# GpSimd in place of VectorE for the low input parts and layer 0's sums, inside a gated recurrence

## The chip, the cores and the metric

The kernel runs on one core of one Trainium2 chip. The metric is the device time of one execution in microseconds (us), taken as the median of several runs; less is better. All times of the profile are microseconds from the start of the span unless ns is written.

## What is computed

Two layers act on x, 4 batches x 512 positions x 256 features. Cut to the part that the change touches:

```
step(h, x_t):                                  # layer 0, a gated recurrence over 512 positions
    z  = sigmoid(x_t W_z + h U_z + vz)
    r  = sigmoid(x_t W_r + h U_r + vr)
    hh = tanh(x_t W + (r * h) U + vh)
    h  = (1 - z) * h + z * hh
hist  = all h                                  # 4 x 512 x 256
blk   = gelu(hist W1 + b1) W2 + b2             # where the router selects the position, else hist
x     = x + (blk or hist)                      # so the kernel needs x + blk and x + hist
x     = x + layer 1 (a 4-expert block, then a 64-expert block, 8 chosen per row)
```

## The kernel before, in words

**Stages.** The program runs in four stages: the recurrence (`gru`, to about 1056 us, with a short set-up before its first step at 21 us), the 4-expert block (`dense`), the routing, and the 64 experts (`experts`, to the end). The change touches `gru` alone.

**The recurrence.** Positions are walked one at a time by a loop over j, on all engines, in 13 windows of 40 steps (the last, window 12, has 32). In the code a window is called a span, and jj is the step's offset in it. The state is feature-major: 128 partitions x 8 values (2 halves of the features x 4 batches). To multiply in half the time a float32 product is split into a high and a low float16 (or float32r) part. One step is a ring of small instructions that wait for each other:

- TensorE (`recur`, L869) makes the r gate's sum from step_high and step_low, the z gate's from the state (`raw`), the candidate's from rh_high and rh_low, and the kept part of the next step's r from keep_part: 48 products of 128x128 by 4 columns. Between them it works through prepared products: one of the next window's input product (L838) at most steps and some of the feed-forward block of the previous window (L882, L897).
- ScalarE forms r (L510), z (L512 to L515) and the candidate (L517), then a larger piece: seeding the next window's banks (L503), GELU, block output (L447), the history copy (L495).
- VectorE forms rh_high (L768) and rh_low (a scan, L630), the kept part (L775, L777, L781), step_high (L785), step_in (L786), step_low (L630), the new state (L794, L799, L801, L805). Each reads two operands in SBUF. After L805 it may do one larger piece that is placed by hand at given offsets.

**The pieces that the change moves.** All are VectorE `tensor_tensor` instructions on one half of the features, [128, 4 batches, 40 positions], placed behind L805 of a step:

- `low_inputs(span, pieces)` (L553 to L556): the low part of the next inputs, x minus its high part, into x_part[1]. In window w the two for window w+2 are made at offsets 7 and 8 (13 and 17 in window 0), behind ScalarE's high part (L420) of offset 4 (10). The two for window 1 are made in the set-up (L569, L570). TensorE waits for them at offset 0 of the window before their own (L945), a whole window after they were made.
- `add_to_block(span, d)` (L701 to L704): blk += x, in window w for w-2, at offsets 36 and 37, behind ScalarE's block output (L447) of offsets 2 and 3. In window 12 at 20, 21 and, for window 11, at 27, 28.
- `add_state(span, d)` (L706 to L710): xT += hist, at offsets 38, 39 (22, 23 and 29, 30 in window 12), behind the adds to the block and the history copies. The results are read in the next stage alone.

There are 24 instructions of each kind, 72 together. `layer_sums` (L712 to L727) holds the offsets of the last two. GpSimd, in this stage, sets six constants at the start (L530 to L537) and is idle until the routing.

The step in which one such piece stands, in VectorE's program:

```
last of the step:  scalar_tensor_tensor(out=part_of(1, j), in0=h_new, ..., in1=part_of(0, j))   # L805
lows = LOW_AT if span else FIRST_LOW_AT                                                         # L807
if span + 2 < SPANS and jj in lows: wait_ge(s_xhi, span + 2); low_inputs(...)                   # L808
ffn_vector(span, jj)                                # sums, hidden splits, weight parts          # L811
next step's first: wait_ge(s_r, m); rh_high = (r + 1) * h                                       # L767
```

Of the kernel before, what the change touches and what calls it, by code (L numbers as in the profile page):

```python
# [6 lines left out]
F32 = mybir.dt.float32  # L7
# [4 lines left out]
ALU = mybir.AluOpType  # L12
# [5 lines left out]
KD = D // P  # L18
# [5 lines left out]
SEG = 16  # L24
# [186 lines left out]
def gru(nc, sem, A, bank, xT, hist, ident, ones, ones_bf, condT, slot_row, s_x, s_const, load_ffn_up, load_ffn_down, load_next,  # L211
        up_loaded, down_loaded, shared_loaded, raw, shared_parts, under, ffn_sems, wr, wr_rep, idle_rows):

    with ExitStack() as own:
        def t(name, shape, dt=F32):
            return own.enter_context(nc.sbuf_tensor(name, shape, dt))

        w16_1, w16_2, h_steps, hid16, full16, blk, x_last, fsc, silu_c, b1, b2 = under
        STARTS = tuple(range(0, S, SPAN))
        LENGTHS = tuple(min(SPAN, S - at) for at in STARTS)  # L220
        SPANS = len(STARTS)
        FINAL = SPANS - 1
# [8 lines left out]
        x_part = [t(f"in_part{p}", [P, KD, B, S], F32R) for p in range(2)]  # L231
# [29 lines left out]
        s_xhi, s_xlo = sem("inputs_high"), sem("inputs_low")  # L261
# [15 lines left out]
        s_hist = sem("hist_copied")  # L277
# [4 lines left out]
        s_fup, s_gelu, s_fhi, s_flo, s_fdn, s_blk = ffn_sems  # L282
        s_silu = sem("cond_silu")
        s_bx = sem("inputs_added_to_block")
# [5 lines left out]
        FIRST_HIGH_AT, FIRST_LOW_AT = TERMS + B, (13, 17)  # L290
        HIGH_AT, LOW_AT = 4, (7, 8)
# [10 lines left out]
        def steps_of(v, span):  # L302
            return v[:, :, :, STARTS[span]:STARTS[span] + LENGTHS[span]]

        def place(j):
            return j // SPAN, j % SPAN
# [39 lines left out]
        ADD_BLOCK_AT, ADD_STATE_AT = (36, 37), (38, 39)  # L346
        ADD_BLOCK_FINAL_AT, ADD_STATE_FINAL_AT = (20, 21), (22, 23)
        ADD_BLOCK_LAST_AT, ADD_STATE_LAST_AT, KEEP_LAST_AT = (27, 28), (29, 30), 20
# [39 lines left out]
        with nc.Block() as block:  # L388
            @block.sync
            def _(sp):  # L390
                for g, (w, u, c, b) in enumerate(names):
                    sp.dma_start(C[:, g], A["L0_cond_" + c].rearrange("(k p) e -> p k e", p=P)).then_inc(s_cw[g], 16)
                for g, (w, u, c, b) in enumerate(names):
                    sp.dma_start(W[:, g], A["L0_cond_" + w].rearrange("(k p) e -> p k e", p=P)).then_inc(s_w[g], 16)
                for g, (w, u, c, b) in enumerate(names):
                    sp.dma_start(U[:, g], A["L0_cond_" + u].rearrange("(k p) e -> p k e", p=P)).then_inc(s_uw, 16)
                load_ffn_up(sp)
                for k in range(KD):
                    sp.dma_start(xT[:, k, :, EARLY:S],
                                 A["xT"][k * P:(k + 1) * P, :].rearrange("p (b s) -> p b s", b=B)[:, :, EARLY:S]).then_inc(s_x, 16)  # L400
                sp.dma_start(slot_row[:], A["slot_row"]).then_inc(s_const, 16)
                load_ffn_down(sp)
                sp.wait_ge(s_x, 32)
                sp.wait_ge(s_const, 16)
                sp.wait_ge(s_w16lo, 2 * PAIRS * LOWS)
                load_next(sp)
# [124 lines left out]
            def _(pool):  # L531
# [4 lines left out]
                nc.gpsimd.memset(idle_rows[:], 0.0)  # L536
                nc.gpsimd.memset(lift[:], 2.0 ** (STATE_EXP - 1)).then_inc(s_set, 1)  # L537

            @block.vector
            def _(dve):  # L540
                nc.vector.memset(ring[:, 2 * SEG - 1], 0.0).then_inc(s_h, 1)
# [8 lines left out]
                dve.sem_inc(s_hr, 1)  # L550
                dve.sem_inc(s_slo, 1)

                def low_inputs(span, pieces):  # L553
                    for k in pieces:
                        nc.vector.tensor_tensor(steps_of(x_part[1], span)[:, k], steps_of(xT, span)[:, k],
                                                steps_of(x_part[0], span)[:, k].bitcast(F32), ALU.subtract).then_inc(s_xlo, 1)  # L556

                def low_weights(g):
                    dve.wait_ge(s_whi, g + 1)
                    nc.vector.tensor_tensor(W_part[1][:, g], W[:, g], W_part[0][:, g].bitcast(F32), ALU.subtract).then_inc(s_wlo, 1)  # L560
# [5 lines left out]
                    last = nc.vector.tensor_reduce(peak[:, g:g + 1], U[:, g].rearrange("p k e -> p (k e)"), AX.X, ALU.max,  # L566
                                                   apply_absolute_value=True)
                last.then_inc(s_peak, 1)
                dve.wait_ge(s_xhi, 1)  # L569
                low_inputs(1, range(KD))  # L570
                dve.wait_ge(s_v, 2)
                nc.vector.tensor_copy(bias[:], bank[1][:, GATES * C2:GATES * C2 + GATES * KD]).then_inc(s_bias, 1)
                dve.wait_ge(s_bias, 1)
# [124 lines left out]
                        nc.vector.scalar_tensor_tensor(out=low, in0=whole, scalar=fsc[:, 13:14], in1=high,  # L698
                                                       op0=ALU.mult, op1=ALU.subtract).then_inc(s_flo, 1)

                def add_to_block(span, d):  # L701
                    dve.wait_ge(s_blk, 2 * KD * span + d + 1)
                    v = steps_of(blk, span)[:, d]
                    nc.vector.tensor_tensor(v, v, steps_of(xT, span)[:, d], ALU.add).then_inc(s_bx, 1)  # L704

                def add_state(span, d):  # L706
                    dve.wait_ge(s_bx, span * KD + d + 1)
                    dve.wait_ge(s_hist, -(-(STARTS[span] + LENGTHS[span]) // SEG))
                    v = steps_of(xT, span)[:, d]
                    nc.vector.tensor_tensor(v, v, steps_of(hist, span)[:, d], ALU.add)  # L710

                def layer_sums(window, jj):  # L712
                    for d in range(KD):
                        if window == FINAL:
                            if jj == ADD_BLOCK_FINAL_AT[d]:
                                add_to_block(window - 2, d)
                            if jj == ADD_STATE_FINAL_AT[d]:
                                add_state(window - 2, d)
                            if jj == ADD_BLOCK_LAST_AT[d]:
                                add_to_block(window - 1, d)  # L720
                            if jj == ADD_STATE_LAST_AT[d]:
                                add_state(window - 1, d)
                        elif window >= 2:
                            if jj == ADD_BLOCK_AT[d]:
                                add_to_block(window - 2, d)
                            if jj == ADD_STATE_AT[d]:
                                add_state(window - 2, d)  # L727

                def ffn_vector(window, jj):
                    layer_sums(window, jj)  # L730
                    if window == 0:
                        scale_step(fsc.bitcast(U32), jj)
                    for f in range(KH):
                        for part in range(2):
                            if window == FINAL and jj == SPLIT_FINAL_AT[f][part]:
                                split_hidden((window - 1) * KH + f, part)
                            if 1 <= window < FINAL and jj == SPLIT_AT[f][part]:
                                split_hidden((window - 1) * KH + f, part)
                    for at in range(2 * PAIRS * LOWS):
                        if (window, jj) == FFN_LOW_AT[at]:  # L740
                            i, n = at // LOWS, at % LOWS
                            whole, high, low = ffn_piece(i, n)
                            c = 6 + i // PAIRS
                            dve.wait_ge(s_w16hi, i + 1)
                            nc.vector.scalar_tensor_tensor(out=low, in0=whole, scalar=fsc[:, c:c + 1], in1=high,
                                                           op0=ALU.mult, op1=ALU.subtract).then_inc(s_w16lo, 1)
                    if (window, jj) in SHARED_LOW_AT:
                        i, n = SHARED_LOW_AT.index((window, jj)) // LOWS, SHARED_LOW_AT.index((window, jj)) % LOWS
                        whole, high, low = shared_piece(i, n * LOW, (n + 1) * LOW)
                        dve.wait_ge(s_nhi, i + 1)  # L750
                        nc.vector.tensor_tensor(low, whole, high.bitcast(F32), ALU.subtract).then_inc(s_nlo, 1)
                    if window == 2 and jj in (21, 22):
                        k = jj - 21
                        nc.vector.tensor_copy(wr_rep[:, k], wr[:, k:k + 1].to_broadcast([P, P]))
                    if (window, jj) == (2, 36):
                        nc.vector.tensor_scalar(half_c[:], condT[:], 0.5, None, ALU.mult).then_inc(s_silu, 1)
                    if (window, jj) == (2, 37):
                        dve.wait_ge(s_silu, 2)
                        nc.vector.scalar_tensor_tensor(out=silu_c, in0=turn_c[:], scalar=1.0, in1=half_c[:],
                                                       op0=ALU.add, op1=ALU.mult).then_inc(s_silu, 1)  # L760

                for j in range(S):
                    h, h_new = ring[:, (j - 1) % (2 * SEG)], ring[:, j % (2 * SEG)]
                    m = j + 1
                    span, jj = place(j)
# [30 lines left out]
                    if j % SEG == 0 and j >= 2 * SEG:  # L796
# [7 lines left out]
                    dve.wait_ge(s_hhi, m + 1)  # L804
                    nc.vector.scalar_tensor_tensor(out=part_of(1, j), in0=h_new, scalar=2.0, in1=part_of(0, j),  # L805
                                                   op0=ALU.mult, op1=ALU.subtract).then_inc(s_hlo, 1)
                    lows = LOW_AT if span else FIRST_LOW_AT  # L807
                    if span + 2 < SPANS and jj in lows:  # L808
                        dve.wait_ge(s_xhi, span + 2)
                        low_inputs(span + 2, (lows.index(jj),))  # L810
                    ffn_vector(span, jj)  # L811
                    if j == 0:
                        low_recurrent(GATES - 1)
# [1206 lines left out]
```

## Time and profile before

| | us |
|---|---|
| median of 3 runs | 2133.65 (2133.19 to 2134.84) |
| the profiled execution: span | 2133.2 |
| the profiled execution: its own time | given by its span alone; it lies 0.45 under the median |
| recurrence (first gate r to the last) | 20.8 to 1053.8 |
| engines busy, share of the span | PE 98%, PEld 92%, DVE 74%, ACT 48%, POOL 19% |

PE is TensorE's matmuls, PEld its weight loads (they overlap), DVE VectorE, ACT ScalarE, POOL GpSimd. A row of the timeline is: start, duration, engine, line, operation, output<-inputs, shapes, count, and in brackets the idle time of the engine before it with what ended it. A row with a count over 1 merges neighbours, so its duration is the stretch that they cover. Pipelined instructions can start before the one ahead has ended.

### The profile page before, as it was taken

The numbers are of one execution on the slowest core, as the hardware profiler recorded it, in microseconds if no ns is written. First come the engines' busy times: TensorE is split into PE (matmuls) and PEld (weight loads), VectorE is DVE, ScalarE is ACT, GpSimd is POOL, SyncE is SP. The second block draws the span as 40 slices with busy tenths as digits, with TensorE's granted clock in tenths as the row PEclk, the third lists the DMA queues.
The fourth block names the chain that finished last, engine by engine and source line by source line (L and its number), as shares of the span: only waits on it lengthen the run. The fifth ranks groups of instructions, "written<-read, shape, count | busy, mean of one in ns | idle before, by whom it ended". The sixth has DMA issues, their size and how long they took to land. (4 is left out here: it accounts for less than half of the span.)

```text
span 2133.2 us, 82927 instructions
## 1 busy us (share of the span) xinstructions
PE 2095.2 (98%) x32732; PEld 1968.5 (92%) x32732; DVE 1572.5 (74%) x8995; ACT 1025.5 (48%) x3981; POOL 415.7 (19%) x560
## 2 busy tenths in 40 slices
PE   8999999999999999999999999999999999999997
PEld 7899999999999999999768888767999999999997
DVE  6887877787777887787745555593777777777775
ACT  3565565665555565656555776533222222222221
POOL 0000000000000000000000000445455555555553
PEclk6555555555555555555599999999999999999998
DMA  3001000000000000000002322223888888888882
GB/s 127 4 4 44 4 4 4 4 4 4 4 4 4 4 4 4 4 4 4 3 1 92 111 84 80 107 70 133 299 268 276 278 267 276 279 268 277 278 264 58
DMA packets 55558, 213.72 MB, mean 100 GB/s; under 512 B 11578, under 2 KB 40960, under 8 KB 46976
## 3 DMA queue, kind: packets, MB, share of 16 engines
q1 hardware_dynamic: 36276, 184.41, 23.5%
q0 software_dynamic: 17408, 23.61, 5.9%
q8 instruction: 257, 4.21, 0.8%
q14 instruction: 133, 1.09, 0.2%
q10 hardware_dynamic: 1484, 0.40, 0.1%
HBM read 192.82 MB, written 15.57 MB: 98 GB/s over the span
## 5 line engine op out<-in xcount | busy, mean ns | idle before, releaser
L1891 PE MATMUL bank<-xe,ring 128*128 128x160 f32 x3072 | 438.8, 299 | 0.7 <-DVE xe L1949 0.7
L1891 PEld LDWEIGHTS bank<-xe,ring 128*128 128x128 f32 x3072 | 422.7, 190 | 0.9 <-issue 0.9
L1942 DVE STREAM_TRANSPOSE turned<-ye 32x64 f32<-32x64 f32 x1240 | 291.5, 235 | 16.2
L869 PEld LDWEIGHTS bank<-keep_part,Us 128*128 128x128 f16 x6120 | 276.0, 111 | 1.6 <-DVE keep_part L781 0.4
L1659 POOL MEMSET cum<- 128x320 f32 x1 | 0.4, 365 | 1349.7 <-POOLq L1051 1349.7
L869 PE MATMUL bank<-keep_part,Us 128*128 128x4 f16 x6120 | 259.3, 170 | 0.4 <-DVE keep_part L781 0.3
L1927 ACT ACTIVATE gate_f<-bank 128x160 f32<-128x160 f32 x384 | 116.4, 303 | 284.7 <-PE bank L1891 283.7
L869 PE MATMUL bank<-raw,Us 128*128 128x4 f16 x6132 | 241.3, 167 | 0.5 <-DVE raw L805 0.4
L1833 POOL DMA_INDIRECT out_rows<-res,to_row x128 | 192.3, 1503 | 227.2 <-DVE res L1961 193.9
L510 ACT ACTIVATE r_h<-bank 128x8 f32<-128x8 f32 x512 | 92.8, 181 | 278.9 <-PE bank L869 278.4
L1902 PE MATMUL bank<-mid,ring 128*128 128x160 f32 x1536 | 219.1, 299 | 0.0
L1902 PEld LDWEIGHTS bank<-mid,ring 128*128 128x128 f32 x1536 | 212.1, 190 | 0.0
L1972 DVE TENSOR_TENSOR mid<-bank,gate_f 128x160 f32<-128x160 f32 x384 | 117.6, 318 | 126.1 <-ACT gate_f L1927 120.3
L869 PEld LDWEIGHTS bank<-raw,Us 128*128 128x128 f16 x6132 | 209.8, 105 | 0.8 <-DVE raw L805 0.6
L869 PE MATMUL bank<-rh_high,Us 128*128 128x4 f16 x4088 | 206.7, 173 | 3.3 <-issue 0.6
L838 PE MATMUL bank<-in_part,W_part 128*128 128x160 f32 (+1 forms) x432 | 206.9, 479 | 1.0 <-DVE bank L612 1.0
L869 PE MATMUL bank<-step_high,Us 128*128 128x4 f16 x4088 | 189.0, 168 | 4.5 <-DVE step_high L785 1.5
L869 PEld LDWEIGHTS bank<-rh_high,Us 128*128 128x128 f16 x4088 | 165.4, 112 | 23.2 <-DVE rh_high L768 11.1
L515 ACT ACTIVATE z_cand<-tz,lift 128x8 f32<-128x8 f32 x512 | 155.8, 304 | 16.5
L869 PEld LDWEIGHTS bank<-step_high,Us 128*128 128x128 f16 x4088 | 148.1, 105 | 9.1 <-DVE step_high L785 3.0
L785 DVE TENSOR_TENSOR step_high<-z_cand 128x8 f16<-128x8 f32 x512 | 89.5, 175 | 81.4 <-ACT z_cand L517 74.5
L1126 PE MATMUL bank<-x_part,weights_part 128*128 128x512 f32 x576 | 137.0, 396 | 2.2 <-DVE x_part L1317 2.2
(279 smaller groups left out, 4051.4 us busy)
## 6 DMA issues: line engine op xcount, KB each, us to landing
ring<-in_ew SPq DMA_DIRECT2D x64, 2304.0 KB, 9.2
raw<-in_L_cond_ew SPq DMA_DIRECT2D x16, 1024.0 KB, 6.2
ctx_rows<-rows SPq DMA_DIRECT2D x2, 1280.0 KB, 7.0
dense_w<-in_L_ffn_W SPq DMA_DIRECT2D x2, 1024.0 KB, 9.3
dense_w<-in_L_cond_sw SPq DMA_DIRECT2D x2, 1024.0 KB, 6.3
out_rows<-res,to_row POOLq DMA_INDIRECT x128, 4.8
xT<-in_xT SPq DMA_DIRECT2D x2, 864.0 KB, 10.7
dense_w<-in_sw1T SPq DMA_DIRECT2D x1, 1536.0 KB, 11.1
```

Source lines behind the costliest of these rows:

```text
L510: nc.scalar.activation(r, pre_of(0, q, jj), ACT.Tanh, scale=inv[0]).then_inc(s_r, 1)
L515: nc.scalar.activation(z, tz[:], ACT.Identity, scale=2.0 ** (STATE_EXP - 1), bias=lift[:, 0:1]).then_inc(s_z, 1)
L785: nc.vector.tensor_tensor(step_high[:, :, 2], z, cand, ALU.mult).then_inc(s_shi, 1)
L838: last = nc.tensor.matmul(product(span, n), W_part[w][:, g, k, m * P:(m + 1) * P], steps_of(x_part[x], span)[:, k], start=(k == 0 and i == ...
L869: last = nc.tensor.matmul(pre[g][q][:, jj, m, :], Us[:, g, p, k, m * P:(m + 1) * P], x[part][:, k * B:(k + 1) * B], start=False, stop=Fals ...
L1126: last = nc.tensor.matmul(up[f % len(up)][:], w[i][:, k, f * P:(f + 1) * P], x[j][:, k], start=(k == 0 and i == 0 and j == 0), stop=(k == ...
L1833: nc.gpsimd.indirect_dma_start(out=out[:, :], out_offset=bass.IndirectOffsetOnAxis(ap=to_idx[c][:, 0:1], axis=0), in_=res[e % 2][c][:], in ...
L1891: last = nc.tensor.matmul(bank[f % UPS][:, s_ * CAP:(s_ + 1) * CAP], w1[u][:, k, s_ * FFN + f * P:s_ * FFN + (f + 1) * P], xe[e % 2][:, k] ...
L1902: last = nc.tensor.matmul(bank[6 + e % 2][:, d * CAP:(d + 1) * CAP], w2[u][:, f, d * P:(d + 1) * P], mid[e % 2][:, f], start=(f == 0), sto ...
L1927: nc.scalar.activation(gate[:, f % 2], bank[f % UPS][:, CAP:2 * CAP], ACT.Silu).then_inc(s_silu, 1)
L1942: last = nc.vector.transpose(y[:, :, q, :], ye[e % 2][q * SQ:(q + 1) * SQ, :, j * SQ:(j + 1) * SQ])
L1972: nc.vector.tensor_tensor(mid[e % 2][:, f], bank[f % UPS][:, 0:CAP], gate[:, f % 2], ALU.mult).then_inc(s_mid, 1)
```

## The change

The 72 instructions go from VectorE's program to GpSimd's, unchanged in operation and shape. On VectorE the waits and pieces at hand-placed offsets disappear. On GpSimd they stand in one loop over windows, in this order: in each window w the two low parts for w+2, then (from w = 2) the two adds to the block and the two adds of the state for w-2; in window 12 those for 10 and for 11. Each is held only by its semaphores, by no offset.

```diff
--- before
+++ after
@@ gpsimd @@
                 nc.gpsimd.memset(lift[:], 2.0 ** (STATE_EXP - 1)).then_inc(s_set, 1)
+                def low_inputs(span):
+                    pool.wait_ge(s_xhi, span)
+                    for k in range(KD):
+                        nc.gpsimd.tensor_tensor(steps_of(x_part[1], span)[:, k], steps_of(xT, span)[:, k],
+                                                steps_of(x_part[0], span)[:, k].bitcast(F32), ALU.subtract).then_inc(s_xlo, 1)
+                def add_to_block(span, d):
+                    pool.wait_ge(s_blk, 2 * KD * span + d + 1)
+                    v = steps_of(blk, span)[:, d]
+                    nc.gpsimd.tensor_tensor(v, v, steps_of(xT, span)[:, d], ALU.add).then_inc(s_bx, 1)
+                def add_state(span, d):
+                    pool.wait_ge(s_bx, span * KD + d + 1)
+                    pool.wait_ge(s_hist, -(-(STARTS[span] + LENGTHS[span]) // SEG))
+                    v = steps_of(xT, span)[:, d]
+                    nc.gpsimd.tensor_tensor(v, v, steps_of(hist, span)[:, d], ALU.add)
+                low_inputs(1)
+                for window in range(SPANS):
+                    if window + 2 < SPANS:
+                        low_inputs(window + 2)
+                    for span in ((window - 2,) if 2 <= window < FINAL else (window - 2, window - 1) if window == FINAL else ()):
+                        for d in range(KD):
+                            add_to_block(span, d)
+                        for d in range(KD):
+                            add_state(span, d)
@@ vector @@
-                def low_inputs(span, pieces): ...
-                dve.wait_ge(s_xhi, 1)
-                low_inputs(1, range(KD))
-                def add_to_block(span, d): ...
-                def add_state(span, d): ...
-                def layer_sums(window, jj): ...
                 def ffn_vector(window, jj):
-                    layer_sums(window, jj)
...
-                    lows = LOW_AT if span else FIRST_LOW_AT
-                    if span + 2 < SPANS and jj in lows:
-                        dve.wait_ge(s_xhi, span + 2)
-                        low_inputs(span + 2, (lows.index(jj),))
                     ffn_vector(span, jj)
```

## Rows read from the trace of the kernel before

**Rows 1.** The page: the span, and TensorE's granted clock in 40 slices.
```profile
span 2133.2 us, 82927 instructions
...
PEclk6555555555555555555599999999999999999998
```

**Rows 2.** Windows, 80 us of recurrence: busy us of each engine (count), granted clock, DMA.
```profile
500.00:580.00 80.00, 79.89 (x2034) 78.62 (x2031) 63.93 (x502) 48.35 (x241) 0.00 (x0) 0.50 0.02 4
```

**Rows 3.** Timeline of window 5, two steps.
```profile
441.68 0.18 ACT L510 ACTIVATE r_h<-bank 128x8 f32<-128x8 f32 x1 [0.57 <-PE bank L869]
441.82 0.29 PEld L838 LDWEIGHTS bank<-in_part,W_part 128*128 128x128 f32 x1
...
441.89 0.17 DVE L768 SCALAR_TENSOR_TENSOR rh_high<-r_h,ring 128x8 f16<-128x8 f32 x1 [0.24 <-ACT r_h L510]
...
442.12 0.33 PEld L869 LDWEIGHTS bank<-rh_high,Us 128*128 128x128 f16 x8
...
442.61 0.55 PEld L869 LDWEIGHTS bank<-keep_part,Us 128*128 128x128 f16 x12
...
442.90 0.18 DVE L785 TENSOR_TENSOR step_high<-z_cand 128x8 f16<-128x8 f32 x1 [0.16 <-ACT z_cand L517]
...
443.13 0.29 PEld L869 LDWEIGHTS bank<-step_high,Us 128*128 128x128 f16 x8
...
443.57 0.32 DVE L555 TENSOR_TENSOR in_part<-xT,in_part 128x160 fp32r<-128x160 f32 x1
443.68 0.18 ACT L510 ACTIVATE r_h<-bank 128x8 f32<-128x8 f32 x1 [0.57 <-PE bank L869]
...
443.89 0.17 DVE L768 SCALAR_TENSOR_TENSOR rh_high<-r_h,ring 128x8 f16<-128x8 f32 x1
...
445.67 0.18 ACT L510 ACTIVATE r_h<-bank 128x8 f32<-128x8 f32 x1 [0.22 <-PE bank L869]
```

**Rows 4.** Groups of VectorE, whole span: busy us, mean ns | idle before.
```profile
L710 DVE TENSOR_TENSOR xT<-xT,hist 128x160 f32<-128x160 f32 x24 | 7.8, 324 | 0.0
L704 DVE TENSOR_TENSOR ffn_out<-ffn_out,xT 128x160 f32<-128x160 f32 x24 | 7.6, 318 | 0.0
L555 DVE TENSOR_TENSOR in_part<-xT,in_part 128x160 fp32r<-128x160 f32 (+1 forms) x24 | 7.5, 316 | 0.0
```

**Rows 5.** Timeline of the routing stage: GpSimd alone, and beside a VectorE instruction.
```profile
1353.04 2.35 POOL L1663 TENSOR_TENSOR context_part<-hist,context_part 128x1024 fp32r<-128x1024 f32 x1 [0.80 <-ACT context_part L1606]
...
1358.43 1.27 POOL L1667 TENSOR_TENSOR shared_part<-dense_w,shared_part 128x512 fp32r<-128x512 f32 x1 [0.57 <-ACT shared_part L1609]
1358.59 1.66 DVE L1711 TENSOR_TENSOR left<-rows,st 128x512 f32<-128x512 f32 x1
...
1364.44 0.69 DVE L1711 TENSOR_TENSOR left<-rows,st 128x512 f32<-128x512 f32 x1
```

**Rows 6.** The same timeline later: both engines with instructions back to back.
```profile
1370.77 1.47 POOL L1676 TENSOR_TENSOR act_f<-act_f,lin 128x512 f32<-128x512 f32 x1
1371.13 1.14 DVE L1725 TENSOR_SCALAR st<-st 128x8 f32<-128x8 f32 x1
1372.21 1.29 POOL L1667 TENSOR_TENSOR shared_part<-dense_w,shared_part 128x512 fp32r<-128x512 f32 x1
...
1372.43 1.61 DVE L1727 TENSOR_TENSOR gates<-gates,left 128x512 f32<-128x512 f32 x1
...
1373.45 1.74 POOL L1676 TENSOR_TENSOR act_f<-act_f,lin 128x512 f32<-128x512 f32 x1
...
1380.89 0.17 DVE L1725 TENSOR_SCALAR st<-st 128x8 f32<-128x8 f32 x1
```

**Rows 7.** Timeline of the set-up, before the first step.
```profile
10.56 0.45 ACT L420 ACTIVATE in_part<-xT 128x320 fp32r<-128x320 f32 x1
...
12.26 1.87 DVE L566 TENSOR_REDUCE peak<-U 128x1 f32<-128x512 f32 x3 [1.70 <-DMA U<-in_L_cond_U]
```

More of the change, by code:

```diff
@@ L551, in _ @@
                 dve.sem_inc(s_slo, 1)
[L553 to L556, printed above, removed]
                 def low_weights(g):
@@ L699, in split_hidden @@
                                                        op0=ALU.mult, op1=ALU.subtract).then_inc(s_flo, 1)
[L701 to L727, printed above, removed]
                 def ffn_vector(window, jj):
-                    layer_sums(window, jj)
                     if window == 0:
```

## The prediction

> **What bounds the kernel now.** I read the page first: the span is 2133.2 us, and TensorE's granted clock is 0.5 to 0.6 for the first 20 of 40 slices [rows 1], which is the 1.2 GHz level; that is the recurrence. Then the busy time by stretch: in 80 us there TensorE is busy 79.89 and its weight loads 78.62, while VectorE is busy 63.93, ScalarE 48.35 and GpSimd nothing [rows 2]. So the recurrence looks bound by TensorE's queue, with VectorE 80% busy and GpSimd free. But a ring of dependent instructions can be as tight as a full queue, and a share doesn't tell which, so I read the timeline of two steps next [rows 3]. A step lasts from one r gate to the next: 441.68 to 443.68 is 2.00 us, 443.68 to 445.67 is 1.99.
>
> Two hand-overs in it decide. **rh_high:** r is ready at 441.68 + 0.18 = 441.86, VectorE's L768 starts at 441.89 and ends at 442.06; TensorE's weight load of the input product ends at 441.82 + 0.29 = 442.11 and rh_high's start at 442.12. So TensorE is the later one, by 0.05. **step_high:** VectorE's L785 ends at 442.90 + 0.18 = 443.08; TensorE's keep_part loads end at 442.61 + 0.55 = 443.16 and step_high's start at 443.13, as one stretch begins while the other is draining. TensorE is later by 0.05 to 0.08; I take 0.05. So TensorE sets the step, but VectorE is only about 0.05 behind it at two places. VectorE waits for data twice in the step, 0.24 before L768 and 0.16 before L785 [rows 3]. These 0.40, and 0.05 at each hand-over, are all the room there is: 0.5 us in a step of 2.0. A VectorE held up for longer holds up the ring, since everything that TensorE could do instead stands behind the waiting product in its own queue.
>
> **The change, part by part.**
>
> *What VectorE loses.* 72 instructions, 24 each of 0.316, 0.318 and 0.324 us [rows 4], 22.9 us in all. What are they worth on the path? L555 at 443.57 ends at 443.89, and L768 behind it starts at 443.89, 0.03 after r (443.86). In the step before, with no such piece, L768 also starts 0.03 after r (441.86 to 441.89), and the two steps take 2.00 and 1.99 [rows 3]. The piece fits exactly into the wait for r. So I take the gain at 0. Its upper bound is the whole 22.9 if no piece were hidden, which the two steps speak against; the lower is nothing.
>
> *What GpSimd gains: its own time.* No row has this instruction at 128x160 on GpSimd. The nearest are the same operation at 1024 columns, 2.35 us, and at 512, 1.27 us, both with no VectorE instruction of two inputs ahead of them [rows 5]. That is 1.08 us for 512 columns, 2.1 ns a column, and 0.19 us at no columns; 160 columns are 0.19 + 0.34 = 0.53 us. Lower bound 0.34 (no fixed part), upper bound the 1.27 of the 512-column row, because four short rows of 40 may run worse than one long row. I take 0.53. GpSimd is idle here, so 72 x 0.53 = 38 us of its time cost nothing by themselves.
>
> The Trainium skill, GPSIMD Engine Reference, section 3.1, gives `tensor_tensor` on GpSimd at 1.96 times VectorE's time. On VectorE's 0.32 [rows 4] that makes an estimate of 0.62, by which the sum below would be 35.7 instead of 29.4 us.
>
> *What it does to VectorE.* This is the term that decides. Where the engines meet in the routing, L1711 takes 0.69 us alone and 1.66 beside a GpSimd instruction: that one ends at 1358.43 + 1.27 = 1359.70, and L1711 ends at 1360.25, 0.55 later. It stood still until GpSimd was done and then ran [rows 5]. A small one fares the same: L1725, 128x8, takes 0.17 alone and 1.14 when issued at 1371.13 beside a GpSimd instruction that ends at 1372.24 [rows 6]. With both queues full they take turns: GpSimd's ends at 1373.50, L1727 runs and ends at 1374.04, and GpSimd's next, issued at 1373.45, takes 1.74 instead of 1.29, having waited 0.45 for it [rows 6]. So one GpSimd instruction holds one VectorE instruction for up to its whole length, and gives way to one in between.
>
> The Trainium skill, SBUF (State Buffer), "Practical consequences", says that a VectorE instruction with two SBUF inputs contends with a GpSimd instruction that reads SBUF, and that the one behind blocks fully. All twelve VectorE instructions of a step are of that kind, though the rows show the hold for `tensor_tensor` and a `tensor_scalar` alone.
>
> *When they run.* On GpSimd nothing is held by an offset. ScalarE's high input part at offset 4 releases the two low parts; the adds to the block wait for block outputs of offsets 2 and 3, already there, and the history copies are long done. So in each of windows 2 to 10 **six instructions run in one burst**, 3.18 us of GpSimd; windows 0 and 1 have bursts of two; window 11 has one at offset 2 and three at offset 3; window 12 twice that pattern. With VectorE's small instructions taking turns, a burst of six meets six to eight of them, about half to one step of its program. Of each burst the room of one step, 0.5 us, is hidden; a lone instruction gets one wait and hand-over of it, about 0.25. The sum:
> - windows 2 to 10: 9 x (3.18 - 0.5) = 24.1
> - windows 0 and 1: 2 x (1.06 - 0.5) = 1.1
> - window 11: (0.53 - 0.25) + (1.59 - 0.5) = 1.4; window 12: 2.8
> - the two of the set-up: 0. ScalarE's part is ready at 10.56 + 0.45 = 11.01, and VectorE waits for a load until 12.26 [rows 7], 1.25 us, which covers 1.06. If that load came early, they would cost up to 1.06.
>
> Together **29.4 us**. With 0.34 us for one it is 70 x 0.34 - 7.7 = 16.1, with 1.27 it is 81.2; 7.7 is the hidden part of the sum.
>
> *Waits added.* GpSimd's waits hold nothing else: behind them in its queue stand only more pieces. TensorE needs the low parts a window (80 us) later, the sums are read after the recurrence, and the last of them can start once the block output at offset 26 of window 12 is done, five steps (10 us) before its end. No DMA moves.
>
> **The number.** The sum is made on the profiled execution: 2133.2 + 29.4 = 2162.6 us. It lies 0.45 under the median of the runs, so I give 2133.65 + 29.4 = 2163.0.
>
> **Rivals.**
> - *A, the forecast: a full hold, taking turns.* 2163. For it: three holds in the rows, among them a 128x8, and a turn given and taken [rows 5, 6]. Chance 0.72.
> - *B, GpSimd gets in only at VectorE's waits.* VectorE's instructions follow each other closely, and GpSimd may only enter where VectorE has stopped for r or for the candidate. Then each holds 0.53 - 0.24 - 0.05 = 0.24 before L768 or 0.53 - 0.16 - 0.05 = 0.32 before L785; 70 times 0.28 is 19.6, a time of 2153. For it: VectorE's queue is denser here than in the rows. Against: between L768 and its scan, before L781 and elsewhere it also stops briefly for its own results. Chance 0.13.
> - *C, not slower: the short instructions aren't held.* If a hold needs VectorE instructions that stream many columns (the only two-input ones in the rows have 512 and more), 8 columns of input may slip through. The place is L768 and L785 beside GpSimd; it decides below a hold of 0.05 to 0.25 an instruction, where the room swallows it. Then the time is 2133.6, and if the removed pieces delayed L768 by 0.03 after all, 70 x 0.03 = 2.1 less, 2131.5. To gain over 0.2% it would need 0.06 for each of 70. The 1.14 of L1725 [rows 6] speaks against. Chance 0.10, of which 0.03 for over 0.2% faster.
> - *D, the piece is dearer on GpSimd.* Past 0.77 us for one (four rows of 40 instead of one) the loss is 70 x 0.77 - 7.7 = 46.2 and more, 2180 or above. Nothing in the rows shows such a shape. Chance 0.05.
>
> **How the numbers follow.** The likeliest is A. The range takes in B and A with prices from about 0.34 to 0.77 for one: 2133.65 + 16.1 is 2149.8, less a few us if a burst hides two steps' room instead of one; 2133.65 + 46.2 is 2179.9. So 2146 to 2180, leaving out C and D. A measurement of this kernel can tell about 0.2%, 4.3 us. Slower by over that: A, B and D, 0.90. Within: 0.07 of C. Faster: 0.03.
>
> **What would show it.** In the profile after: GpSimd busy by some 38 us more, 72 instructions at 0.53 or a little longer for waiting their turn; six in a row after offset 4 of windows 2 to 10; beside them VectorE's small instructions at 0.5 to 0.7 us instead of 0.17; one or two steps per window that take 2.7 us longer together, and all others at 2.00. VectorE's summed busy time would rise, not fall. The stages after the recurrence keep their length. Wrong if L768, L785 and the scans keep 0.17 to 0.21 us beside GpSimd (C), if only those behind a wait grow (B), or if a burst is much over 4.2 us long (D). If steps free of GpSimd's work fall clearly below 1.99 us where a piece stood, the removed pieces were not hidden, and my zero for the gain was wrong.

## The result: 12.7 us slower, and the profile after

The changed kernel takes 2146.22 us (median of 4 runs, 2145.77 to 2149.28) against 2133.49 for the kernel before. The ratio is 1.0059, with a 95% interval of 1.0047 to 1.0071: 12.7 us slower, where 29.4 were forecast. The direction was right, the size more than twice too large, and the median stands at the very bottom of the range.

The page of the kernel after, with the lines that answer to [rows 1]:

```profile
span 2147.5 us, 82919 instructions
...
PEclk6555555555555555555599999999999999999998
```

This execution was the longest of the four, 2149.28 us, so 1.8 us lie outside its span. (In runs of the kernel before it is 2.0; so the execution profiled before took about 2135.2 us and lay over the median, not 0.45 under it, which the forecast, made from the median, does not hang on.) Its span is 14.3 us longer than that of before. By the L510 rows the recurrence runs from 20.94 to 1067.98, 1047.04 us, against 20.83 to 1053.80, 1032.97: 14.1 of the 14.3 us are in the recurrence. The clock there is still the lower of the two levels.

The runs of the kernel before lie near two levels, 2131 and 2134.5 us, so beside each median below I also give the length of the recurrence in the profiled execution (1032.97 before, 1047.04 after). It is the steadier measure: no version changes anything behind the recurrence, yet the rest of the span lies anywhere between 1096.0 and 1101.2 us in the twelve traces.

Window, as [rows 2], and the groups of GpSimd that took the place of [rows 4]:

```profile
500.00:580.00 80.00, 79.34 (x2014) 77.33 (x2012) 63.12 (x489) 46.94 (x235) 2.98 (x6) 0.50 0.02 4
```

```profile
L554 POOL TENSOR_TENSOR xT<-xT,hist 128x160 f32<-128x160 f32 x24 | 12.3, 531 | 0.0
L542 POOL TENSOR_TENSOR in_part<-xT,in_part 128x160 fp32r<-128x160 f32 (+1 forms) x24 | 12.2, 525 | 821.5 <-ACT in_part L420 821.5
L548 POOL TENSOR_TENSOR ffn_out<-ffn_out,xT 128x160 f32<-128x160 f32 x24 | 12.1, 518 | 201.1 <-ACT ffn_out L447 201.1
```

GpSimd's price was read rightly: 0.518 to 0.531 us each against 0.53, although each instruction here works on four short rows of 40 columns. In these 80 us VectorE gave up 0.8 us of busy time, not the six pieces' 1.9, although half a step less fell into them: the instructions beside GpSimd grew. Over the whole span its busy time went from 1572.5 to 1573.7 us, so 22.9 us of pieces left and as much came back.

This is the burst of window 5, timeline of VectorE, ScalarE's r gate, GpSimd and some weight loads, as [rows 3]. The step before it takes 1.99, the one behind it 2.03.

```profile
442.27 1.03 POOL L542 TENSOR_TENSOR in_part<-xT,in_part 128x160 fp32r<-128x160 f32 x2 [78.80 <-ACT in_part L420]
442.34 0.50 DVE L792 SCALAR_TENSOR_TENSOR r_h<-keep,step_in 128x8 f32<-128x8 f32 x1
...
442.65 0.18 ACT L510 ACTIVATE r_h<-bank 128x8 f32<-128x8 f32 x1 [0.46 <-PE bank L856]
442.76 0.15 DVE L796 SCALAR_TENSOR_TENSOR raw<-ring,raw 128x8 f16<-128x8 f32 x1
442.86 0.47 DVE L759 SCALAR_TENSOR_TENSOR rh_high<-r_h,ring 128x8 f16<-128x8 f32 x1
442.97 0.19 PEld L856 LDWEIGHTS bank<-raw,Us 128*128 128x128 f16 x4 [0.23 <-DVE raw L796]
...
443.26 0.99 POOL L548 TENSOR_TENSOR ffn_out<-ffn_out,xT 128x160 f32<-128x160 f32 x2
...
443.36 0.48 DVE L650 TENSOR_TENSOR_SCAN rh_low<-r_h,rh_high 128x24 f16<-128x24 f32 x1
...
443.77 0.52 DVE L766 SCALAR_TENSOR_TENSOR keep_part<-nz,ring 128x8 f16<-128x8 f32 x1
...
444.21 0.15 DVE L768 SCALAR_TENSOR_TENSOR keep<-nz,ring 128x8 f32<-128x8 f32 x1
...
444.23 1.02 POOL L554 TENSOR_TENSOR xT<-xT,hist 128x160 f32<-128x160 f32 x2
...
444.47 0.31 DVE L772 TENSOR_TENSOR keep_part<-keep,keep_part 128x8 f16<-128x8 f32 x1
444.70 0.16 DVE L776 TENSOR_TENSOR step_high<-z_cand 128x8 f16<-128x8 f32 x1
444.78 0.50 DVE L777 SCALAR_TENSOR_TENSOR step_in<-z_cand 128x8 f32<-128x8 f32 x1
...
445.45 0.18 PEld L856 LDWEIGHTS bank<-step_low,Us 128*128 128x128 f16 x4 [0.22 <-DVE step_low L650]
...
445.75 0.18 ACT L510 ACTIVATE r_h<-bank 128x8 f32<-128x8 f32 x1 [1.36 <-PE bank L856]
```

Six GpSimd instructions in a row, six VectorE instructions grown: L792, L759, the scan, L766, L772 and L777, by 0.34, 0.30, 0.27, 0.35, 0.14 and 0.34 over the 0.16, 0.17, 0.21, 0.17, 0.17 and 0.16 that they take elsewhere. That makes **1.74 us of holds, 0.29 each**. The step from 442.65 to 445.75 takes 3.10 and the next 2.03, so 1.13 us of the 1.74 reach the step and 0.6 are hidden. In windows 3 to 9 the step of offset 5 takes 3.10 or 3.11, in window 10, with short last inputs, 2.91. A held instruction ends just behind GpSimd's: GpSimd's second, fourth and sixth end at 443.30, 444.25 and 445.25, and L759, L766 and L777 at 443.33, 444.29 and 445.28. Between two held instructions others run at full speed: L796, L768 and L776 each end within 0.15 or so of the start of GpSimd's next. GpSimd isn't slowed by them: six in a row take 442.27 to 445.25, 0.50 each.

### The profile page after: what moved, and what is told of

The parts are those of the page before. It is cut to its first block and busy times, and to the rows that moved or that the text cites. A ratio compares the mean times of both kernels' runs of the same rounds, so it can differ in the third digit from the quotient of the medians.

```text
span 2147.5 us, 82919 instructions
## 1 busy us (share of the span) xinstructions
PE 2101.3 (98%) x32724; PEld 1969.6 (92%) x32732; DVE 1573.7 (73%) x8923; ACT 1025.5 (48%) x3981; POOL 451.5 (21%) x632
## 5 line engine op out<-in xcount | busy, mean ns | idle before, releaser
L510 ACT ACTIVATE r_h<-bank 128x8 f32<-128x8 f32 x512 | 92.7, 181 | 284.4 <-PE bank L856 283.9
L542 POOL TENSOR_TENSOR in_part<-xT,in_part 128x160 fp32r<-128x160 f32 (+1 forms) x24 | 12.2, 525 | 821.5 <-ACT in_part L420 821.5
L776 DVE TENSOR_TENSOR step_high<-z_cand 128x8 f16<-128x8 f32 x512 | 89.0, 174 | 78.9 <-ACT z_cand L517 70.5
```

Of the source, the lines that this page charges most:

```text
L510: nc.scalar.activation(r, pre_of(0, q, jj), ACT.Tanh, scale=inv[0]).then_inc(s_r, 1)
L776: nc.vector.tensor_tensor(step_high[:, :, 2], z, cand, ALU.mult).then_inc(s_shi, 1)
```

## The experiments

The kernel before took 2133.98 us (24 runs) beside the sums alone, the low parts alone, the halves and the run without sums; 2131.63 (13 runs) beside the merged pairs, the copies and the run released by L794; and 2134.45 (17 runs) beside the memsets and the two runs released by L805.

**The parts alone.** First the sums alone on GpSimd (low parts back at their offsets on VectorE):

```diff
-                low_inputs(1)                      # GpSimd
                 for window in range(SPANS):
-                    if window + 2 < SPANS:
-                        low_inputs(window + 2)
```

> Only the 48 sums go to GpSimd; the low parts of the inputs stay on VectorE. Theory 1 (GpSimd's instruction holds VectorE's port only for its column part, about 0.34 of its 0.53 us; what isn't swallowed by the room in a step lengthens it): windows 2 to 11 each have one instruction at offset 2 and three at offset 3, as window 11 of the changed kernel, which lost about 1.1 us; 10 x 1.1 and 2.0 in window 12 make 13 us over the kernel before. Theory 2 (the whole 0.53 us holds, and more is hidden than I counted, some 2 us of every burst): a burst of three or four, 1.6 to 2.1 us, is hidden all but whole; 0 to 4 us over before.

Measured: 2144.41 us, ratio 1.0042 (1.0025 to 1.0059), 10.4 us over before; recurrence 1042.97, 10.0 over: nearer to theory 1's 13 than to theory 2's 0 to 4. Then the low parts alone (`layer_sums` back on VectorE):

```diff
                     if window + 2 < SPANS:
                         low_inputs(window + 2)     # GpSimd
-                    for span in (...): add_to_block, add_state
```

> Only the 24 low parts of the inputs go to GpSimd, two behind each other in windows 0 to 10; the sums stay on VectorE at their offsets. Theory 1: 2 x 0.34 less little; window 1 of the changed kernel, with the same two, lost 0.6; 11 x 0.6 is 7 us over before. Theory 2 (2 us of a burst hidden): 1.06 us is hidden whole, 0 to 1 us over before.

Measured: 2136.68, ratio 1.0013 (1.0003 to 1.0023), 2.7 us over; recurrence 1038.21, 5.2 over (the rest of this execution's span is 3.3 us shorter than that of before). The sums carry most of the loss: one instruction at the end of offset 2 makes the step of offset 3 2.28, and the three behind it make the step of offset 4 2.81 in windows 4 to 9, 1.1 us together. Two low parts make one step 2.28 in windows 3 to 9, and 2.48 to 2.62 in windows 1, 2 and 10. So in most windows a pair costs 0.3, four 1.1 and six 1.1: not additive. For the low parts alone theory 1 had said 7 us and theory 2 at most 1; the recurrence lies between them. Why a pair is cheap is seen in this timeline of the run with low parts alone, window 5 (next r gates at 440.36 and 442.64, as the step is 2.28):

```profile
439.98 1.03 POOL L542 TENSOR_TENSOR in_part<-xT,in_part 128x160 fp32r<-128x160 f32 x2 [79.64 <-ACT in_part L420]
440.04 0.50 DVE L816 SCALAR_TENSOR_TENSOR r_h<-keep,step_in 128x8 f32<-128x8 f32 x1
...
440.46 0.15 DVE L820 SCALAR_TENSOR_TENSOR raw<-ring,raw 128x8 f16<-128x8 f32 x1
440.57 0.47 DVE L783 SCALAR_TENSOR_TENSOR rh_high<-r_h,ring 128x8 f16<-128x8 f32 x1
...
440.78 0.29 PEld L849 LDWEIGHTS bank<-in_part,W_part 128*128 128x128 f32 x1
```

The first hold, 0.34, makes the state's low part (L820) late, and with it TensorE, whose queue has reached the input product 0.3 late (440.78). The second hold, 0.30 on rh_high, ends at 441.04, before that product's load is done at 441.07. Two holds fall on two sides of the same 0.3 and are paid once.

**What holds: GpSimd's time or its columns.** Each instruction cut in two, over two batches each:

```diff
-    for k in range(KD): tensor_tensor(...[:, k], ...)
+    for k in range(KD):
+        for b in range(0, B, 2): tensor_tensor(...[:, k, b:b + 2], ...)    # all three kinds; TensorE waits for twice the count
```

> The changed kernel with each GpSimd instruction cut in two of two batches (80 columns, about 0.36 us each by the intercept of 0.19): the same columns in 144 instructions. Theory 1 (hold by columns, the fixed part free): the loss stays near 12.7 us, at most a few us less. Theory 2 (whole instruction holds): GpSimd's time of a burst of six grows from 3.2 to 4.3 us, and the loss with it to about 24 us.

Measured: 2140.57, ratio 1.0031 (1.0020 to 1.0041), 6.6 us over; recurrence 1041.37, 8.4 over. Timeline of its window 5, in part (GpSimd at 439.68, 440.96 and 442.26, four in each row), and the group:

```profile
439.68 1.32 POOL L543 TENSOR_TENSOR in_part<-xT,in_part 128x80 fp32r<-128x80 f32 x4 [77.40 <-ACT in_part L420]
...
439.75 0.33 DVE L795 SCALAR_TENSOR_TENSOR r_h<-keep,step_in 128x8 f32<-128x8 f32 x1
...
440.73 0.30 DVE L769 SCALAR_TENSOR_TENSOR keep_part<-nz,ring 128x8 f16<-128x8 f32 x1
...
442.60 0.36 DVE L762 SCALAR_TENSOR_TENSOR rh_high<-r_h,ring 128x8 f16<-128x8 f32 x1
```

```profile
L543 POOL TENSOR_TENSOR in_part<-xT,in_part 128x80 fp32r<-128x80 f32 (+1 forms) x48 | 15.7, 355 | 808.5 <-ACT in_part L420 808.5
```

GpSimd works 30% longer (47.4 us in the three groups against 36.6), and the loss of a burst halves: two steps of 2.32 and 2.28 instead of 3.10 and 2.03. In the whole recurrence it falls from 14.1 to 8.4 us. Theory 2 falls. Theory 1 has the sign, but promised "a few us less" at most. The other way, each pair made one of 320 columns (`add_to_block` and `add_state` over both halves at once):

> The changed kernel with each pair of GpSimd instructions made one over both feature halves (320 columns, about 0.87 us by 0.19 + 320 x 0.0021): the same columns in 36 instructions. Theory 1 (hold by columns): three holds of 0.68 instead of six of 0.34, loss near 12.7 us or a few us above, since a long hold overruns the room. Theory 2 (whole instruction holds): GpSimd's time of a burst falls from 3.2 to 2.6 us, and the loss to about 7 us.

Measured: 2149.63, ratio 1.0079 (1.0062 to 1.0096), 18.0 us over the 2131.63 beside it (15.6 over 2134); recurrence 1048.36, 15.4 over. GpSimd's three groups together are shorter (31.3 us) and the loss is a little larger, not near theory 2's 7 us. The timeline of window 5:

```profile
442.68 0.89 POOL L541 TENSOR_TENSOR in_part<-xT,in_part 128x320 fp32r<-128x320 f32 x1 [79.05 <-ACT in_part L420]
...
442.80 0.80 DVE L793 SCALAR_TENSOR_TENSOR raw<-ring,raw 128x8 f16<-128x8 f32 x1
```

The hold is 0.80 - 0.17 = 0.63. With 80, 160 and 320 columns GpSimd's instruction takes 0.36, 0.53 and 0.87 us and holds a short VectorE instruction for up to 0.19, 0.35 and 0.68. **The hold is at most its length less 0.16 to 0.19**: in the traces with GpSimd's `tensor_tensor` in the recurrence a held short instruction ends 0.02 to 0.07 behind GpSimd's, so nearly all of its own 0.17 passes under the hold. The same columns in smaller portions fit better between the waits.

**Reading or any work.** On the kernel before, six copies of 160 columns (one input) in windows 0 to 10, then in their place six memsets:

```diff
+for window in range(SPANS - 2):
+    pool.wait_ge(s_xhi, window + 2)
+    for i in range(6):
+        ...                                        # waits for the last but one of its own writes
+        nc.gpsimd.tensor_copy(spare[:, n % 2], C[:, 0, 0, 0:160])     # second run: memset(spare[:, n % 2], 0.0)
```

> The kernel before, with six copies of 160 float32 columns on GpSimd (one input) in the same places. If the hold is for reading: VectorE's instructions beside them are held, by less than for two inputs, since the copy is shorter; some us over before. If only two-input instructions of GpSimd hold: 2133.5.

Measured: 2137.58, ratio 1.0019 (1.0009 to 1.0029); recurrence 1035.64, 2.7 over; the step of offset 5 takes 2.30 in most windows.

> The kernel before, with six memsets of 320 bfloat16 columns on GpSimd (about 0.35 us each, they read nothing) to a spare tile behind ScalarE's high input part in windows 0 to 10, beside the six copies of the run before, 0.32 us each with one input, which lengthened the step of offset 5 by 0.30. If the hold is for reading the state buffer: no such step, 2.00 there, and the time of the kernel before. If any work of GpSimd, its writes or its semaphores hold VectorE: again 0.3 us a window.

Measured: 2134.43, ratio 0.9998 (0.9989 to 1.0007); recurrence 1034.41. Its 1.4 us over before are not at offset 5, where the step takes 2.00 against 1.99 to 2.00: they are a few thousandths of a us in each of hundreds of steps, most of them without memsets, and their cause is open. These memsets have 320 columns, as a tile for 384 did not fit into SBUF and that version gave no time. First the copies, then the memsets:

```profile
439.93 0.57 POOL L547 COPY spare<-C 128x160 f32<-128x160 f32 x2
439.96 0.30 DVE L785 SCALAR_TENSOR_TENSOR keep_part<-nz,ring 128x8 f16<-128x8 f32 x1
440.19 0.34 DVE L787 SCALAR_TENSOR_TENSOR keep<-nz,ring 128x8 f32<-128x8 f32 x1
```

```profile
437.82 0.97 POOL L546 MEMSET spare<- 128x320 bf16 x3
437.87 0.17 DVE L784 SCALAR_TENSOR_TENSOR keep_part<-nz,ring 128x8 f16<-128x8 f32 x1
437.95 0.16 DVE L786 SCALAR_TENSOR_TENSOR keep<-nz,ring 128x8 f32<-128x8 f32 x1
```

Beside copies VectorE's instructions grow by 0.13 and 0.18; beside memsets, which write as many bytes, they keep 0.17 and 0.16. So GpSimd's reads hold VectorE, its writes, waits and semaphores don't. The Trainium skill, SBUF (State Buffer), "Practical consequences", says just this of a VectorE instruction with two SBUF inputs and GpSimd's reads and writes; the trace agrees, for instructions of 8 columns too.

**Where in the step.** Every GpSimd instruction in a step of its own, at VectorE's old offsets, released by L794 (L785 in the changed kernel) of that step; then released by L805; then by L805 in halves, at offsets 7 to 10 and 30 to 37 (in window 12 elsewhere, the last eight two a step):

```diff
-    (six in a row as their data come)
+    for each step with a piece:
+        pool.wait_ge(s_hhi, j + 2)        # L794's; then s_hlo, L805's; then s_hlo with halves, each in a step of its own
+        one piece
```

> The changed kernel with every GpSimd instruction put into a step of its own, at the offsets that VectorE had, released by the step's L785 (s_hhi), so that it runs from about 1.75 us into the step, over VectorE's wait for r. Theory 1 (the column part at the end holds): it starts about 0.45 before the next rh_high, so it holds VectorE 0.05 to 0.1 beyond it, of which 0.05 is room; 70 x 0.05 is 3 us over before. Theory 2 (whole instruction holds from its start): L792 and L796 are held too, and the loss is near that of 70 lone instructions, 0.2 each, 14 us.

Measured: 2155.27, ratio 1.0106 (1.0090 to 1.0123); recurrence 1053.43, 20.5 over, more than either theory had (3 and 14 us). It is the slowest of all: steps of 2.34 behind the low parts and the last of the sums, 2.26 behind the others.

```profile
449.83 0.52 POOL L542 TENSOR_TENSOR in_part<-xT,in_part 128x160 fp32r<-128x160 f32 x1 [16.12 <-DVE raw L795]
...
449.86 0.51 DVE L806 SCALAR_TENSOR_TENSOR raw<-ring,raw 128x8 f16<-128x8 f32 x1
...
450.43 0.18 PEld L866 LDWEIGHTS bank<-raw,Us 128*128 128x128 f16 x4 [0.28 <-DVE raw L806]
```

L794 is followed so closely by the rest that GpSimd started just before the state's low part was issued. That instruction (L805 before, L806 here), which I had counted as free, is the one held (0.51 for 0.17), and TensorE stands 0.28 us for it.

> The changed kernel with every GpSimd instruction (160 columns) in a step of its own, released by the step's last VectorE instruction (L805, s_hlo) rather than by L794. Theory 1, put now as: VectorE's instruction is held until GpSimd's ends, less the 0.15 to 0.2 us that it takes anyway. GpSimd's starts at about 0.04 after L805's end and ends 0.53 later, some 0.2 after the place where rh_high would have ended; less 0.05 of room that is 0.15 for each, 10 us in all; steps of 2.15 to 2.2. The state's low part is not held, as it was in the run released by L794 (steps of 2.34). If the hold ended before the instruction does, the steps stay at 2.00 to 2.05.

Measured: 2146.70, ratio 1.0059 (1.0044 to 1.0074); recurrence 1047.79, 14.8 over, where 10 had been expected. Steps with a piece take 2.20, as expected, or 2.13 in window 10; the others take what they take in the changed kernel.

```profile
449.44 0.17 DVE L806 SCALAR_TENSOR_TENSOR raw<-ring,raw 128x8 f16<-128x8 f32 x1
449.64 0.18 ACT L510 ACTIVATE r_h<-bank 128x8 f32<-128x8 f32 x1 [0.57 <-PE bank L866]
449.69 0.52 POOL L542 TENSOR_TENSOR in_part<-xT,in_part 128x160 fp32r<-128x160 f32 x1 [16.00 <-DVE raw L806]
...
449.85 0.39 DVE L769 SCALAR_TENSOR_TENSOR rh_high<-r_h,ring 128x8 f16<-128x8 f32 x1 [0.24 <-ACT r_h L510]
```

GpSimd ends at 450.21 and rh_high at 450.24, where it would have ended at 450.02: held 0.22, less a little room, 0.20 a step as expected.

> The same with each instruction cut in two of 80 columns (0.36 us), each half in a step of its own behind L805. Theory 1: a half ends about where rh_high would have ended, 0.24 us of VectorE's wait for r cover it; the steps stay at 2.00 to 2.03, the time within 0.1% of the kernel before although GpSimd does all 72 pieces in 144 instructions. If each GpSimd instruction had a price of its own whatever its place (semaphores, dispatch), 144 of them would cost more than the 72 of the changed kernel, 13 us and over. No version is expected to beat the kernel before by more than 0.1%, as the pieces were hidden there too.

Measured: 2139.97, ratio 1.0028 (1.0017 to 1.0039), 5.5 us over; recurrence 1038.69, 5.7 over. The steps of offsets 8 to 11, behind the low parts, take 2.03 or 2.04, as expected. Those of offsets 31 and 33 take 2.11 instead of their usual 2.03: there VectorE still has a larger piece behind L805, and GpSimd's half takes 0.43 and ends later. I had not multiplied either: 140 halves at 0.04 on average are the 5.7 us that "within 0.1%" left out. In the rows of offset 7 GpSimd starts 0.08 after L805's end, not 0.04, and rh_high takes 0.23 instead of 0.17.

```profile
445.94 0.36 POOL L542 TENSOR_TENSOR in_part<-xT,in_part 128x80 fp32r<-128x80 f32 x1 [20.00 <-DVE raw L803]
...
446.10 0.23 DVE L766 SCALAR_TENSOR_TENSOR rh_high<-r_h,ring 128x8 f16<-128x8 f32 x1 [0.24 <-ACT r_h L510]
```

**What removal from VectorE is worth.** The kernel before without the sums anywhere (`layer_sums(window, jj)` deleted):

> The kernel before without the 48 sums of layer 0 (no adds to the block or to the state; this part is left out on every engine). Both theories: the pieces were hidden on VectorE, so the time stays at that of the kernel before within 0.1%. If it falls by 5 us or more, my zero for the gain is wrong and the loss on the other side is larger than 12.7 us.

Measured: 2130.78, ratio 0.9986 (0.9976 to 0.9995), 3.2 us less; recurrence 1030.96, 2.0 less: a little more than the 0.1% that was allowed for. The median step at offsets 36 to 39, where the sums stood, is 2.01 with and without them. So the sums are hidden in their steps, and what is gained is small and lies elsewhere, in the steps of 2.1 to 2.3 that are scattered over the recurrence of every run.

These steps go with VectorE's program, not with GpSimd's work. Over windows 1 to 12 the same 25 steps are over 2.09 in the three kernels that have VectorE's program of before (before, copies, memsets). In the six that have that of the changed kernel, whatever GpSimd does, the same 29 are in all six, of which only 4 are among those 25; without the sums anywhere there are 16. In several of them VectorE stands idle for 0.22 to 0.30 us for nothing that the profile shows. This is the step of offset 7 of window 5, which takes 2.34, in the changed kernel and in the one released by L805:

```profile
447.93 0.17 DVE L796 SCALAR_TENSOR_TENSOR raw<-ring,raw 128x8 f16<-128x8 f32 x1 [0.30 <-issue]
```

```profile
447.45 0.17 DVE L806 SCALAR_TENSOR_TENSOR raw<-ring,raw 128x8 f16<-128x8 f32 x1 [0.30 <-issue]
```

Why VectorE stops there is open. But the six kernels allow a sum that leaves GpSimd out: each step at the shortest that it takes in any of them adds up to a recurrence of 1033.12, against 1032.97 before. So by this estimate taking the pieces from VectorE gained nothing, and 13.9 of the 14.1 us are lost in steps that GpSimd lengthens.

## Why the prediction had the direction right and the size wrong

- **TensorE sets the step, VectorE close behind; the removed pieces gain nothing.** Right: by the estimate above the recurrence without them, and without GpSimd's work, is as long as before to 0.15 us. The run without the sums gained 2.0 us there, but not in their steps.
- **GpSimd's own time, 0.53 us.** Right: 0.518 to 0.531. The rival of a dearer piece and the estimate of 0.62 from the Trainium skill's ratio (GPSIMD Engine Reference, section 3.1) were both too high; the ratio is 0.53 / 0.32 = 1.65 here.
- **It holds VectorE, six in a burst, at offset 5, and two or fewer steps carry it.** Right. `scalar_tensor_tensor`, the scan and a `tensor_tensor` of 8 and 24 columns are held, so the rival in which short instructions slip through is out, and so is the one in which GpSimd gets in only at VectorE's waits: L766 and L777 were held in the middle of a run of instructions. That one or two VectorE instructions run between two held ones is right too, but in the burst GpSimd does not wait for them, as it did for L1727 [rows 6].
- **The step that failed** is the term for what one costs: "one GpSimd instruction holds one VectorE instruction for up to its whole length". I charged 0.53 for each and took 0.5 of room off once a burst: 3.18 - 0.5 = 2.68. The trace shows 0.29 for each on average, at most 0.35, 1.74 a burst, of which 0.6 are hidden: 1.13. The room was nearly right; the hold was mis-sized by 0.24 for each of six. It was there to be read in [rows 5]: L1711 ended 0.55 after GpSimd's end though it takes 0.69 alone, so 0.14 of its own time had passed under the hold. Of a 0.69 us instruction that is a detail; of a 0.17 us one it is nearly all. [rows 6] had the small case itself: the 128x8 L1725, 0.17 alone, ends at 1371.13 + 1.14 = 1372.27, only 0.03 after GpSimd's end at 1372.24. So a full block, as the prediction had it, adds less to a short instruction than GpSimd's whole length. With a hold of 0.53 - 0.17 = 0.36 my own sum would have been 70 x 0.36 - 7.7 = 17.5 us, 1.4 times what came. What remains above 12.7 is in part that one (L772) began when GpSimd's was half over, held by 0.14 alone, and in part, as argued from the pair of low parts, that two holds in a burst can fall on the two sides of one hand-over.
- **Room.** I found two hand-overs and missed the third, the state's low part (L805) to TensorE. Held by 0.34, it costs 0.25 to 0.34, as the run released by L794 shows. It is why spreading the instructions out, one a step, doesn't help unless each starts behind L805.
- **Elsewhere.** By windows, the difference in the trace is 9.2 us in windows 2 to 10 and 4.8 in the other four. I had 24.1 and 5.3. Without the scattered steps, by the estimate above, it is 10.1 and 3.8.

## What to carry to other kernels

When an elementwise piece goes to GpSimd beside short two-input VectorE instructions on the critical ring, price each at its length on GpSimd less one short VectorE instruction at most, then ask which VectorE instruction it will land on; its share of busy time says nothing. Work that fits into a wait of its own engine is best left there: 0.32 us behind the last instruction of a step cost next to nothing on VectorE, and the same piece on GpSimd cost 0.15 (in a pair) to 0.34 wherever it was put whole, and 0.04 on average for each half behind L805. No version here that does all the work beat the kernel before.

## What the runs showed that I had not expected

- The hold on a short instruction is shorter than GpSimd's instruction by 0.16 us or more, as the held one ends 0.02 to 0.07 behind GpSimd's: at most 0.19 of 0.36, 0.35 of 0.53, 0.68 of 0.87.
- Cutting the same columns into halves lowered the loss from 12.7 to 6.6 us (in the recurrence from 14.1 to 8.4), although GpSimd's time rose by 30%.
- GpSimd's `tensor_tensor` follows one line, 0.19 us and 2.1 ns a column, from 80 to 1024 columns (0.36, 0.53, 0.87, 1.27 and 2.35 us), also where the columns lie in several rows of 40.
- Six instructions in a burst cost 0.19 us each, and one alone between L794 and L805 0.25 to 0.34: a lone one is not the cheaper.
- Steps of 2.1 to 2.3 stand at the same places in all kernels with the same VectorE program and move when that program changes; why is open.
